# Cross-attention of a small transformer block: two phases with one softmax per row, in place of a running softmax

## The chip, the cores and the metric

The kernel runs on one core of one Trainium2 chip. A core has a matrix engine (TensorE, PE in the rows), a vector engine (VectorE, DVE), an activation engine (ScalarE, ACT), GpSimd (POOL) and SyncE (SP), which here only issues DMAs. The engines run their own instruction streams in order and meet at semaphores. The metric is the device time of one execution in microseconds (us). Before the change it was 133.56 us, the median of 3 runs (132.82 to 136.61).

## The reference, cut to what matters

```python
def _L0_xattn_ref(query, value):                      # 256 queries, 4096 keys, width 256
    scores = jnp.einsum('bqd,bkd->bqk', query, value)
    distribution = jax.nn.softmax(scores, axis=-1)
    return jnp.einsum('bqk,bkd->bqd', distribution, value)

x = x + _L0_xattn_ref(_layernorm(x, axis=-1), ctx_1024)
x = x + _L0_attn_ref(_layernorm(x, axis=-1), L0_attn_w_attn, L0_attn_w_proj)   # 16 heads, causal, position biases
x = x + _L0_ffn_ref(_layernorm(x, axis=-1), L0_ffn_Wg, L0_ffn_W1, L0_ffn_W2, L0_ffn_W3)  # 8 experts
```

`ctx_1024` is 4096 rows of 256 numbers and serves as keys and as values. The change concerns the first of the three lines.

## The kernel before, in words

All data is fp32. The 256 queries are two blocks b of 128 rows, the 4096 keys are eight chunks i of 512. For accuracy each fp32 operand of a product is split into a high part (`_hi`, rounded to the format fp32r that the matrix engine takes in one pass) and a rest (`_lo` = operand - high part), and a product is three matmuls: hi x hi, hi x lo, lo x hi. A tile (i, b) is one chunk against one block. It costs:

- PE: `scores_of` (L837 to L848), 6 matmuls of 512 columns; `transpose_of` (L850 to L857), 4 transposes of the probabilities; `values_of` (L859 to L870), 12 matmuls of 256 columns.
- ACT: `exps` (L692 to L700), exponentials of the scores with the running maximum, with their row sum, and a one-column exponential `shrink` by which older sums must be scaled; `hi_of` (L702 to L708), the high part of the transposed probabilities. Once per chunk also the high part of keys (`split_k`, L674) and of values (`split_v`, L679).
- DVE: `next_max` (L466 to L472), a maximum of the tile and its merge into the running maximum; `lo_of` (L454 to L459); `next_out` (L480 to L491), which rescales the row sum `denom` (L485) and the accumulator `acc` (L490).
- POOL: the low parts of keys and values, `split_lo` (L361 to L370), one instruction each per chunk.

PE, ACT, DVE and POOL each go through the chunks in an order written out by hand, with hardware loops (`Fori`) in the middle. In PE's loop (L886) the scores are one chunk ahead of the values: transpose (i,0), values (i-1,1), scores (i+1,0), transpose (i,1), values (i,0), scores (i+1,1). Two PSUM banks hold scores, two hold transposes, two hold chunk outputs.

All loads are on SP's queue. Keys `kT` and values `v_sb` of all eight chunks have their own space, so their loads (L294 to L304) wait only for the load before them; then come the weights of the later stages (L305 to L314), the 4 MB of `wup_sb` among them. Behind the cross-attention stand `add_attention` (divide, add to x), the statistics of the next layer norm (`norm_stats`, its `rstd` on POOL, `norm_apply`), and the causal attention, whose position biases `bias[:, h]` are 16 multiplications of 128x384 on DVE (`bias_heads`, L445): 3 at the start, 4 after the last `norm_apply`, 5 between the two halves of `mask_k(0, .)` and 4 inside the attention. POOL and DVE share the masking of keys per head (L394 and L552).

Of the kernel before, what the change touches and what calls it, by code (L numbers as in the profile page):

```python
# [9 lines left out]

# [5 lines left out]
FP32 = mybir.dt.float32  # L16
# [5 lines left out]
P = 128  # L22
# [4 lines left out]
L = NCH - 1  # L27
# [17 lines left out]
WARM_BEFORE_NORM_1 = 3  # L45
# [4 lines left out]

EARLY_BIASES, MORE_BIASES, LATE_BIASES = 3, 7, 12
# [15 lines left out]
def build(nc, x, ctx_t, ctx_v, w_qkv, w_proj, w_gate, w_up, w_down, out):  # L67
    es = ExitStack()
    with es:
        def sb(name, shape, dtype=FP32):  # L70
            return es.enter_context(nc.sbuf_tensor(name, shape, dtype))

        def carve(region, size, pattern, **axes):

            part = region[0][:, region[1]:region[1] + size]
            region[1] += size
            return part.rearrange(pattern, **axes)

# [36 lines left out]
        k_lo = sb("k_lo", [P, 2, KC, CH], FP32R)
        v_hi = sb("v_hi", [P, 2, NT, C], FP32R)
        v_lo = sb("v_lo", [P, 2, NT, C], FP32R)
        p_hi = sb("p_hi", [P, TB, NT, P], FP32R)
        p_lo = sb("p_lo", [P, TB, NT, P], FP32R)


        before_up = [wup_sb[:, 4:8].rearrange("p e w k h -> p (e w k h)"), 0]
        before_dn = [wdn_sb[:, 4:8].rearrange("p e k c -> p (e k c)"), 0]
        over_v = [v_sb[:, :, :, :].rearrange("p i n c -> p (i n c)"), 0]
        bias = carve(before_up, NH * 3 * P, "p (h k) -> p h k", h=NH)
        probs = before_up[0][:, before_up[1]:before_up[1] + TB * CH].rearrange("p (b k) -> p b k", b=TB)
        biased = carve(before_up, 3 * 512, "p (s k) -> p s k", s=3)
        aprobsT = carve(before_dn, 2 * 4 * 3 * P, "p (s h m q) -> p s h m q", s=2, h=4, m=3)

        y_T = carve(before_dn, NO * T, "p (o t) -> p o t", o=NO)  # L130
        kM = carve(over_v, NH * T, "p (h k) -> p h k", h=NH)
        k_plain = carve(over_v, 2 * T, "p (m t) -> p m t", m=2)


        UW = 32 * NH // 2
        vpad = carve(over_v, TB * 2 * (UW + HD), "p (k n) -> p k n", k=TB)
        v_slots = [vpad[:, b].rearrange("p (u n) -> p u n", u=2)[:, :, 0:UW].rearrange(
            "p u (m d) -> p u m d", d=32)[:, :, :, 0:HD] for b in range(TB)]
        aprobs = carve(over_v, 3 * 512, "p (s k) -> p s k", s=3)
        q_T = carve(over_v, 2 * T, "p (m t) -> p m t", m=2)  # L140
# [23 lines left out]
        weighted = carve(over_v, TB * E * CAP, "p (b n) -> p b n", b=TB)  # L164
        scatter = carve(over_v, EG * TB * P, "p (g b t) -> p g b t", g=EG, b=TB)
        xg_T = carve(over_v, KC * E * CAP, "p (k n) -> p k n", k=KC)
        act = carve(over_v, EG * H, "p (g h) -> p g h", g=EG)
        h_T = carve(over_v, EG * KH * P, "p (g k n) -> p g k n", g=EG, k=KH)
        y_e = carve(over_v, EG * C, "p (g c) -> p g c", g=EG)
        x_out = carve(over_v, TB * C, "p (b c) -> p b c", b=TB)  # L170
# [3 lines left out]
        s_bank, t_bank, o_bank = banks[0:2], banks[4:6], banks[6:8]  # L174
# [22 lines left out]
        first_kT_loaded = sem("first_kT_loaded")  # L197
        first_v_loaded = sem("first_v_loaded")
        kT_loaded = sem("kT_loaded")
        v_loaded = sem("v_loaded")  # L200
# [16 lines left out]
        scores_ready = sem("scores_ready")  # L217
        chunkmax_ready = sem("chunkmax_ready")
        negmax_ready = sem("negmax_ready")
        probs_ready = sem("probs_ready")  # L220
        shrink_ready = sem("shrink_ready")
        probsT_in_psum = sem("probsT_in_psum")
# [910 lines left out]
```

## Time and profile before

| | before |
|---|---|
| median of 3 runs | 133.56 us (132.82 to 136.61) |
| span of the profiled execution | 134.4 us |
| first score matmul to end of last values matmul | 7.24 to 70.95 us |
| one chunk in the loop | 7.20 us |
| busy in the span: PE, DVE, ACT, POOL | 117.0, 96.3, 68.1, 56.5 us |

The profile is one execution. Starts and durations of instructions are in us from the start of the span; a matmul's duration overlaps the next one's, so the pace of matmuls is read from the distance of their starts. "Idle before" is how long an engine did nothing ahead of an instruction, and behind the arrow stands what it waited for last.

### The profile page before, as it was taken

The numbers are of one execution on the slowest core, as the hardware profiler recorded it, in microseconds if no ns is written. First come the engines' busy times: TensorE is split into PE (matmuls) and PEld (weight loads), VectorE is DVE, ScalarE is ACT, GpSimd is POOL, SyncE is SP. The second block draws the span as 40 slices with busy tenths as digits, with TensorE's granted clock in tenths as the row PEclk, the third lists the DMA queues.
The fourth block names the chain that finished last, engine by engine and source line by source line (L and its number), as shares of the span: only waits on it lengthen the run. The fifth ranks groups of instructions, "written<-read, shape, count | busy, mean of one in ns | idle before, by whom it ended". The sixth has DMA issues, their size and how long they took to land.

```text
span 134.4 us, 2666 instructions
## 1 busy us (share of the span) xinstructions
PE 117.0 (87%) x838; PEld 87.9 (65%) x838; DVE 96.3 (72%) x260; ACT 68.1 (51%) x171; POOL 56.5 (42%) x56
## 2 busy tenths in 40 slices
PE   5990599998989898998896999998999898799982
PEld 5770489896969697887794956554467577534540
DVE  0899566798988979798958887998867489410312
ACT  3470745866757483938421439989690320415100
POOL 2599075292948577585501799500000330300000
PEclk9999779999999999999999999999999999999999
DMA  4998878879999100059000000000057989300002
GB/s 133 356 369 251 273 274 294 258 226 304 429 441 468 68 0 0 0 156 454 22 0 0 2 0 0 0 5 2 0 141 322 458 351 444 166 0 0 0 5 78
DMA packets 3754, 22.69 MB, mean 169 GB/s; under 512 B 544, under 2 KB 800, under 8 KB 3232
## 3 DMA queue, kind: packets, MB, share of 16 engines
q1 hardware_dynamic: 3744, 22.55, 44.6%
q8 instruction: 6, 0.10, 0.3%
q14 instruction: 4, 0.03, 0.1%
HBM read 22.29 MB, written 0.26 MB: 168 GB/s over the span
## 4 chain that ended last, share of the span: by engine, by line
DVE 45%; PE 30%; ACT 10%; issue 8%; DMA 2%; POOL 2%; ACTq 1%; DVEq 1%
DVE denom L485 7%; DVE wup_sb L448 7%; PE bank L1047 5%; DVE negmax L471 5%; DVE chunkneg L468 3%; ACT p_hi L707 3%; PE bank L918 3%; PE bank L1062 3%; DVE v_sb L552 3%; DVE wup_sb L563 2%; ACT v_sb L768 2%; PE bank L948 2%; DVE acc L490 2%; DMA x_sb<-x_in 2%; PE bank L965 2%
## 5 line engine op out<-in xcount | busy, mean ns | idle before, releaser
L365 POOL TENSOR_TENSOR k_lo<-wdn_sb,k_hi (+1 forms) x7 | 16.9, 2414 | 16.1 <-ACT k_hi L677 16.0
L369 POOL TENSOR_TENSOR v_lo<-v_sb,v_hi (+1 forms) x8 | 19.5, 2441 | 4.1 <-ACT v_hi L682 4.1
L696 ACT ACTIVATE wup_sb<-bank,negmax 128x512 f32<-128x512 f32 x16 | 11.0, 687 | 16.7 <-DVE negmax L471 11.7
L866 PE MATMUL bank<-v_hi,p_hi 128*128 128x256 f32 (+1 forms) x64 | 19.4, 303 | 0.0
L867 PE MATMUL bank<-v_lo,p_hi 128*128 128x256 f32 (+1 forms) x64 | 18.0, 282 | 0.0
L868 PE MATMUL bank<-v_hi,p_lo 128*128 128x256 f32 (+1 forms) x64 | 18.0, 282 | 0.0
L855 PE MATMUL bank<-ident,wup_sb 128*128 128x128 f32 x64 | 10.5, 289 | 7.6 <-ACT wup_sb L696 7.6
L332 POOL TENSOR_TENSOR rstd<-vareps,power 128x1 f32<-128x1 f32 x6 | 3.4, 573 | 29.7 <-DVE vareps L422 29.6
L855 PEld LDWEIGHTS bank<-ident,wup_sb 128*128 128x128 f32 x64 | 7.6, 146 | 12.0 <-ACT wup_sb L696 10.9
L457 DVE TENSOR_TENSOR p_lo<-bank,p_hi 128x512 fp32r<-128x512 f32 x16 | 11.0, 686 | 6.3 <-ACT p_hi L707 6.3
L768 ACT ACTIVATE v_sb<-wup_sb,nmax 128x128 f32<-128x128 f32 (+1 forms) x32 | 14.1, 443 | 2.2 <-DVE nmax L563 2.2
L828 PE MATMUL bank<-ident 128*128 128x128 f32 x86 | 13.0, 309 | 1.7 <-POOL ident L326 1.6
L828 PEld LDWEIGHTS bank<-ident 128*128 128x128 f32 x86 | 12.1, 218 | 2.3 <-POOL ident L326 1.6
L844 PE MATMUL bank<-k_hi,q_hi 128*128 128x512 f32 (+1 forms) x32 | 13.4, 418 | 0.0
L707 ACT ACTIVATE p_hi<-bank 128x512 fp32r<-128x512 f32 x16 | 9.5, 593 | 7.2 <-PE bank L855 7.1
L845 PE MATMUL bank<-k_lo,q_hi 128*128 128x512 f32 (+1 forms) x32 | 13.1, 409 | 0.0
L846 PE MATMUL bank<-k_hi,q_lo 128*128 128x512 f32 (+1 forms) x32 | 13.0, 405 | 0.0
L918 PE MATMUL bank<-v_sb 128*128 128x512 f32 x24 | 12.3, 601 | 0.2 <-DVE v_sb L552 0.2
L866 PEld LDWEIGHTS bank<-v_hi,p_hi 128*128 128x128 f32 x64 | 12.3, 192 | 0.2 <-DVE p_lo L457 0.2
L867 PEld LDWEIGHTS bank<-v_lo,p_hi 128*128 128x128 f32 x64 | 12.2, 191 | 0.0
L868 PEld LDWEIGHTS bank<-v_hi,p_lo 128*128 128x128 f32 x64 | 12.1, 190 | 0.0
L485 DVE SCALAR_TENSOR_TENSOR denom<-denom,shrink,rowsum 128x1 f32<-128x1 f32 x14 | 11.2, 797 | 0.0
(120 smaller groups left out, 236.9 us busy)
## 6 DMA issues: line engine op xcount, KB each, us to landing
wup_sb<-w_up SPq DMA_DIRECT2D x2, 4096.0 KB, 14.6
wdn_sb<-ctx_t SPq DMA_DIRECT2D x8, 512.0 KB, 4.1
v_sb<-ctx_v SPq DMA_DIRECT2D x8, 512.0 KB, 4.5
wdn_sb<-w_down SPq DMA_DIRECT2D x2, 2048.0 KB, 10.6
wqkv_sb<-w_qkv SPq DMA_DIRECT2D x1, 768.0 KB, 7.2
x_sb<-x_in SPq DMA_DIRECT2D x1, 256.0 KB, 2.8
wproj_sb<-w_proj SPq DMA_DIRECT2D x1, 256.0 KB, 7.3
x_out_dram<-v_sb SPq DMA_DIRECT2D x2, 128.0 KB, 1.8
```

The costliest lines, as they stand in the source:

```text
L365: nc.gpsimd.tensor_tensor(k_lo[:, i % 2], kT[:, i], k_hi[:, i % 2].bitcast(FP32), ALU.subtract).then_inc(k_lo_ready, 1)
L369: nc.gpsimd.tensor_tensor(v_lo[:, i % 2], v_sb[:, i], v_hi[:, i % 2].bitcast(FP32), ALU.subtract).then_inc(v_lo_ready, 1)
L485: nc.vector.scalar_tensor_tensor(denom[:, b:b + 1], denom[:, b:b + 1], shrink[:, b, bass.ds(i, 1)], rowsum[:, b, bass.ds(i, 1)], ALU.mult, ...
L707: nc.scalar.activation(p_hi[:, b].rearrange("p n q -> p (n q)"), t_bank[b][:, :], ACT.Copy).then_inc(p_hi_ready, 1)
L768: last = nc.scalar.activation(aprobs[:, n % 3, m * keys:(m + 1) * keys], biased[:, n % 3, m * keys:(m + 1) * keys], ACT.Exp, bias=nmax[:, ...
L828: nc.tensor.matmul(bank[:, 0:P], ident[:, :], ident[:, :], start=True, stop=True)
L844: nc.tensor.matmul(s_bank[b][:, :], q_hi[:, k, cols], k_hi[:, i % 2, k], start=(k == 0), stop=False)
L855: last = nc.tensor.transpose(t_bank[b][:, n * P:(n + 1) * P], probs[:, b, n * P:(n + 1) * P], ident[:, :])
L866: nc.tensor.matmul(o_bank[b][:, 0:C], p_hi[:, b, n], v_hi[:, i % 2, n], start=(n == 0), stop=False)
L867: nc.tensor.matmul(o_bank[b][:, 0:C], p_hi[:, b, n], v_lo[:, i % 2, n], start=False, stop=False)
L868: last = nc.tensor.matmul(o_bank[b][:, 0:C], p_lo[:, b, n], v_hi[:, i % 2, n], start=False, stop=(n == NT - 1))
L918: nc.tensor.matmul(as_bank[n % 3][:, :], q_T[:, h // HPT, b * P:(b + 1) * P], kM[:, h:h + len(heads), 0:keys], start=True, stop=True).then ...
```

## The change

The cross-attention becomes two phases. In the first, PE makes all 16 score tiles; ACT copies each from PSUM to SBUF (`keep_scores`), where all of them stay (`scores_sb`), and DVE takes the tile's maximum from SBUF (`chunk_max`). `row_max` reduces the eight maxima of a block to one. In the second phase ACT writes exponentials over the kept scores with that one maximum, and the value products of all chunks add up in one PSUM bank per block. `v_hi` has two more columns, ones and zeros, so that the row sum is column 256 of the product. `shrink`, `denom` and `acc`, the merging of maxima and the row sums are gone. `S_TILES` and `P_TILES` give the order of tiles in the phases.

Work moves between engines: low parts of keys and values go from POOL to DVE (`split_k_lo`, `split_v_lo`), the high part of values from ACT to POOL (`split_v_hi`), all 16 bias multiplications from DVE to POOL. Keys pass through three input buffers (KB), values through two (`v_in`), and the split values through four (VB); the transposes have three PSUM banks and three `p_hi`/`p_lo` buffers (PB). Values from chunk 2 on are loaded behind the weights, and the later weights are loaded earlier than before. The loops are unrolled, and the second norm's transpose of block 0 stands before the last values tile, in place of three warming matmuls.

```diff
@@ constants
+S_TILES = [(i, b) for i in range(NCH - 2) for b in range(TB)] + [(i, b) for b in range(TB) for i in (NCH - 2, NCH - 1)]
+P_TILES = [(0, 0), (1, 0)] + [t for i in range(2, NCH) for t in ((i, 0), (i - 2, 1))] + [(NCH - 2, 1), (NCH - 1, 1)]
+SB, PB, KB, VB = 4, 3, 3, 4
...
@@ SyncE
-            for i in range(2, NCH):
-                sync.wait_ge(kT_loaded, (i - 1) * 16)
-                sync.dma_start(kT[:, i], ctx_t[i]).then_inc(kT_loaded, 16)
-                sync.wait_ge(v_loaded, (i - 1) * 16)
-                sync.dma_start(v_sb[:, i], ctx_v[i]).then_inc(v_loaded, 16)
+            for i in range(KB, NCH):
+
+                sync.wait_ge(k_lo_ready, i - KB + 1)
+                sync.dma_start(k_in[:, i % KB], ctx_t[i]).then_inc(k_loaded[i % KB], 16)
             sync.dma_start(wqkv_sb[:, :, :], w_qkv).then_inc(wqkv_loaded, 16)
...
+            sync.dma_start(wup_lo[:, :, :, :, :], w_up[:, 0:4]).then_inc(wup_loaded[0], 16)
+            for i in range(2, NCH):
+
+                sync.wait_ge(v_lo_ready, i - 1)
+                sync.dma_start(v_in[:, i % 2], ctx_v[i]).then_inc(v_loaded[i % 2], 16)
...
@@ GpSimd
+            def split_v_hi(i):
+                pool.wait_ge(v_loaded[i % 2], 16 * (i // 2 + 1))
+                if i >= VB:
+
+                    pool.wait_ge(values_ready, P_AT[i - VB, 1] + 1)
+                nc.gpsimd.tensor_copy(v_hi[:, i % VB, :, 0:C], v_in[:, i % 2]).then_inc(v_hi_ready, 1)
+
+            pool.wait_ge(rel_ready, 2)
+            for i in range(2):
+                split_v_hi(i)
+            bias_heads(0, 10)
+            for i in range(2, NCH):
+                split_v_hi(i)
+                bias_heads(8 + i, 9 + i)
...
@@ VectorE
+            def chunk_max(i, b):
+                n = S_AT[i, b]
+                dve.wait_ge(scores_kept_s, n + 1)
+                nc.vector.tensor_reduce(chunkneg[:, b, i:i + 1], scores_sb[:, b, i], AX.X, ALU.max,
+                                        negate=True).then_inc(chunkmax_ready, 1)
...
+            for i in range(NCH - 2):
+                split_k_lo(i + 1)
+                for b in range(TB):
+                    chunk_max(i, b)
+            split_k_lo(NCH - 1)
+            chunk_max(NCH - 2, 0)
+            split_v_lo(0)
+            chunk_max(NCH - 1, 0)
+            row_max(0)
+            chunk_max(NCH - 2, 1)
+            split_v_lo(1)
+            chunk_max(NCH - 1, 1)
+            row_max(1)
+            lo_of(*P_TILES[0])
+            for h in range(1, TB * NCH):
+                if h % 2 and (h + 3) // 2 < NCH:
+                    split_v_lo((h + 3) // 2)
+                lo_of(*P_TILES[h])
...
@@ ScalarE
+            for i in range(NCH - 2):
+                split_k_hi(i + 2)
+                for b in range(TB):
+                    keep_scores(i, b)
+            keep_scores(NCH - 2, 0)
+            keep_scores(NCH - 1, 0)
+            exps(*P_TILES[0])
+            exps(*P_TILES[1])
+            keep_scores(NCH - 2, 1)
+            exps(*P_TILES[2])
+            hi_of(*P_TILES[0])
+            keep_scores(NCH - 1, 1)
...
@@ TensorE
+            for h in range(TB * NCH):
+                values_of(*P_TILES[h])
+                if h + PB < TB * NCH:
+                    transpose_of(*P_TILES[h + PB])
+                if h == TB * NCH - 2:
+                    norm_T(1, 0)
```

What this does to the order of work is seen best on two engines. DVE before, from the first tile of its loop body (a bracket names the semaphores that an instruction waits for; ISA and REGISTER_ALU rows are the loop's register work):

```order
L457 TENSOR_TENSOR p_lo<-bank,p_hi 128x512 [waits p_hi_ready]
L482 ISA
L483 REGISTER_ALU [waits shrink_ready]
L485 ISA [waits denom_ready,probs_ready]
L485 SCALAR_TENSOR_TENSOR denom<-denom,shrink,rowsum 128x1
L490 SCALAR_TENSOR_TENSOR acc<-acc,shrink,bank 128x256 [waits acc_ready,chunk_out_ready]
L467 ISA
L468 TENSOR_REDUCE chunkneg<-bank 128x1 [waits scores_ready]
L470 REGISTER_ALU
L471 ISA [waits chunkmax_ready]
L471 TENSOR_TENSOR negmax<-chunkneg,negmax 128x1
```

DVE now, from the end of the first phase into the second (L476 and L482 are the low parts of keys and values, L488 a tile's maximum, L493 the row's, L498 the low part of probabilities):

```order
L476 TENSOR_TENSOR k_lo<-k_in,k_hi 128x1024 [waits k_hi_ready]
L488 TENSOR_REDUCE chunkneg<-scores_sb 128x1 [waits scores_kept_s]
L482 TENSOR_TENSOR v_lo<-v_in,v_hi 128x1024 [waits v_hi_ready]
L488 TENSOR_REDUCE chunkneg<-scores_sb 128x1 [waits scores_kept_s]
L493 TENSOR_REDUCE negmax<-chunkneg 128x1 [waits chunkmax_ready]
L488 TENSOR_REDUCE chunkneg<-scores_sb 128x1 [waits scores_kept_s]
L482 TENSOR_TENSOR v_lo<-v_in,v_hi 128x1024 [waits v_hi_ready]
L488 TENSOR_REDUCE chunkneg<-scores_sb 128x1 [waits scores_kept_s]
L493 TENSOR_REDUCE negmax<-chunkneg 128x1 [waits chunkmax_ready]
L498 TENSOR_TENSOR p_lo<-bank,p_hi 128x512 [waits p_hi_ready]
L482 TENSOR_TENSOR v_lo<-v_in,v_hi 128x1024 [waits v_hi_ready]
L498 TENSOR_TENSOR p_lo<-bank,p_hi 128x512 [waits p_hi_ready] x2
```

The rescaling is gone from a tile, the split of a chunk's keys or values has come in, and the low part of the second tile of the phase stands behind the low part of value chunk 2.

POOL before, its loop over chunks and what stood behind it:

```order
L365 TENSOR_TENSOR k_lo<-wdn_sb,k_hi 128x1024
L369 ISA [waits v_hi_ready]
L369 ISA
L369 TENSOR_TENSOR v_lo<-v_sb,v_hi 128x1024
L378 REGISTER_ALU
L378 COMPARE_AND_BRANCH
```

POOL now, in the same stretch (L403 is the high part of a value chunk, L396 one bias multiplication):

```order
L403 CAST v_hi<-v_in 128x4x256 [waits v_loaded1]
L396 TENSOR_SCALAR bias<-rel 128x384 x10
L403 CAST v_hi<-v_in 128x4x256 [waits v_loaded0]
L396 TENSOR_SCALAR bias<-rel 128x384
L403 CAST v_hi<-v_in 128x4x256 [waits v_loaded1]
L396 TENSOR_SCALAR bias<-rel 128x384
L403 CAST v_hi<-v_in 128x4x256 [waits values_ready,v_loaded0]
```

Two subtractions per chunk have left POOL; a copy per chunk and the bias multiplications have come, and from chunk 4 on the copy waits for PE's values.

## Rows read from the trace of the kernel before

**Rows 1.** By stretch: length, busy us PE PEld DVE ACT POOL, clock, DMA, GB/s.
```profile
33.20:40.40 7.20, 6.72 (x46) 5.81 (x45) 6.30 (x11) 4.79 (x11) 4.80 (x2) 1.00 1.02 416
...
16.00:18.00 2.00, 2.00 (x6) 1.41 (x6) 0.69 (x1) 1.12 (x2) 0.80 (x1) 0.50 0.81 297
```

**Rows 2.** Timeline, one loop turn: start, duration, instruction, idle before it.
```profile
35.99 2.44 POOL L369 TENSOR_TENSOR v_lo<-v_sb,v_hi  x1
...
36.46 0.28 PE L867 MATMUL bank<-v_lo,p_hi 128*128 x1
...
36.58 0.28 PE L868 MATMUL bank<-v_hi,p_lo 128*128 x1
...
37.24 1.21 DVE L471 TENSOR_TENSOR negmax<-chunkneg,negmax 128x1 f32 x1 [0.19 <-DVE chunkneg L468]
...
38.61 0.69 ACT L696 ACTIVATE wup_sb<-bank,negmax 128x512 f32<-128x512 f32 x1 [1.74 <-DVE negmax L471]
```

**Rows 3.** Chain that ended last: start, us; four transposes and one score matmul.
```profile
21.78 0.44 PE bank L855 x4
23.64 0.23 PE bank L844
```

**Rows 4.** Groups by line and shape: count, busy us, mean ns, idle before.
```profile
L457 DVE TENSOR_TENSOR p_lo<-bank,p_hi 128x512 fp32r<-128x512 f32 x16 | 11.0, 686 | 6.3 <-ACT p_hi L707 6.3
L468 DVE TENSOR_REDUCE chunkneg<-bank 128x1 f32<-128x512 f32 x14 | 9.5, 680 | 2.2 <-PE bank L846 2.2
...
L707 ACT ACTIVATE p_hi<-bank 128x512 fp32r<-128x512 f32 x16 | 9.5, 593 | 7.2 <-PE bank L855 7.1
...
L677 ACT ACTIVATE k_hi<-wdn_sb 128x1024 fp32r<-128x1024 f32 x3 | 3.2, 1053 | 2.7 <-DMA wdn_sb<-ctx_t 2.7
```

**Rows 5.** Timeline of the start.
```profile
6.18 0.67 DVE L437 TENSOR_TENSOR k_lo<-wdn_sb,k_hi 128x512 fp32r<-128x512 f32 x1
...
7.24 0.49 PE L844 MATMUL bank<-k_hi,q_hi 128*128 128x512 f32 x1
...
8.43 2.55 DVE L448 TENSOR_SCALAR wup_sb<-rel 128x384 f32<-128x384 f32 x1
...
10.72 2.47 POOL L369 TENSOR_TENSOR v_lo<-v_sb,v_hi 128x1024 fp32r<-128x1024 f32 x1
...
14.88 0.66 PE L855 MATMUL bank<-ident,wup_sb 128*128 128x128 f32 x4 [4.59 <-ACT wup_sb L696]
```

**Rows 6.** SP's issue of value chunk 2; issue to landing of the 4 MB loads.
```profile
9.34 0.33 SPq L304 DMA_DIRECT2D v_sb<-ctx_v  x1
...
DMA to landing us min/median/max: 12.6/14.6/16.6
```

**Rows 7.** POOL: a memset by group; the masking line's min/median/max ns.
```profile
L384 POOL MEMSET v_sb<- 128x1088 f32 x1 | 1.0, 1012 | 0.1
...
L394 POOL TENSOR_SCALAR v_sb<-v_sb,headmask x16: 598/606/1101, 75.2 to 85.2; 128x128 f32<-128x128 f32 x16
```

**Rows 8.** Timeline behind the cross-attention.
```profile
70.67 0.28 PE L868 MATMUL bank<-v_hi,p_lo 128*128 128x256 f32 x1
...
72.45 0.48 DVE L526 SCALAR_TENSOR_TENSOR x_sb<-acc,rdenom,x_sb 128x256 f32<-128x256 f32 x1
...
73.88 0.55 POOL L332 TENSOR_TENSOR rstd<-vareps,power 128x1 f32<-128x1 f32 x1 [1.98 <-DVE vareps L422]
74.47 0.41 DVE L427 TENSOR_SCALAR xn<-x_sb,meanvar,rstd 128x256 f32<-128x256 f32 x1 [0.67 <-POOL rstd L332]
...
74.80 1.25 DVE L448 TENSOR_SCALAR wup_sb<-rel 128x384 f32<-128x384 f32 x4
...
76.78 1.60 DVE L448 TENSOR_SCALAR wup_sb<-rel 128x384 f32<-128x384 f32 x5
...
77.43 0.38 ACT L754 ACTIVATE v_sb<-bank 128x256 f32<-128x256 f32 x1 [0.51 <-PE bank L935]
...
87.54 1.15 DVE L448 TENSOR_SCALAR wup_sb<-rel 128x384 f32<-128x384 f32 x4
```

More of the change, by code:

```diff
@@ L115, in build @@
[L115 to L125, printed above, removed]
@@ new lines, in build, with carve @@
+        room = region(KB * KC * CH)
+        k_in = at("k_in", [P, KB, KC, CH], room)
+        p_hi = at("p_hi", [P, PB, NT, P], room, FP32R)
+        p_lo = at("p_lo", [P, PB, NT, P], room + PB * CH * 4, FP32R)
+        split_probs = room
+        room = region(VB * NT * (2 * C + 2))
+        v_hi = at("v_hi", [P, VB, NT, C + 2], room, FP32R)
+        v_lo = at("v_lo", [P, VB, NT, C], room + VB * NT * (C + 2) * 4, FP32R)
+        over_v_first = room
+        over_v = [over_v_first]
+        def carve(name, shape, region_at):
+            first = region_at[0]
+            region_at[0] += (math.prod(shape[1:]) * 4 + 63) // 64 * 64
+            return at(name, shape, first)
@@ L196, in build @@
         x_loaded = sem("x_loaded")
[L197 to L200, printed above, removed]
+        k_loaded = [sem(f"k_loaded{j}") for j in range(KB)]
+        v_loaded = [sem(f"v_loaded{j}") for j in range(2)]
         wqkv_loaded = sem("wqkv_loaded")
@@ L443, in _, with split_k_lo @@
                                         ALU.subtract).then_inc(q_lo_ready, 1)
-            def bias_heads(first, end):
-                for h in range(first, end):
-                    nc.vector.tensor_scalar(bias[:, h], rel[:, :], SLOPES[h], None, ALU.mult)
-            dve.wait_ge(rel_ready, 2)
-            bias_heads(0, EARLY_BIASES)
+            def split_k_lo(i):
+                dve.wait_ge(k_hi_ready, i + 1)
+                nc.vector.tensor_tensor(k_lo[:, i % KB], k_in[:, i % KB], k_hi[:, i % KB].bitcast(FP32),
+                                        ALU.subtract).then_inc(k_lo_ready, 1)
@@ L834, in _, with scores_half @@
             keep_warm(banks[7], WARM_BEFORE_SCORES)
[L837 to L839 removed]
+            def scores_half(i, b, k):
+                n = S_AT[i, b]
                 cols = slice(b * P, (b + 1) * P)
[L841 to L848 removed]
@@ new lines, in scores_half, with room_for_scores @@
+                nc.tensor.matmul(s, q_hi[:, k, cols], k_lo[:, i % KB, k], start=False, stop=False)
+                last = nc.tensor.matmul(s, q_lo[:, k, cols], k_hi[:, i % KB, k], start=False, stop=(k == KC - 1))
+                if k == KC - 1:
+                    last.then_inc(scores_in_psum, 1)
+            def room_for_scores(i, b):
+                n = S_AT[i, b]
+                pe.wait_ge(k_lo_ready, i + 1)
+                if n >= SB:
+                    pe.wait_ge(scores_kept_s, n - SB + 1)
@@ new lines, in transpose_of, with values_of @@
+            def transpose_of(i, b):
+                h = P_AT[i, b]
+                pe.wait_ge(probs_ready, h + 1)
+                if h >= PB:
+                    pe.wait_ge(p_lo_ready, h - PB + 1)
+                for n in range(NT):
+                    last = nc.tensor.transpose(t_bank[h % PB][:, n * P:(n + 1) * P],
+                                               scores_sb[:, b, i, n * P:(n + 1) * P], ident[:, :])
+                last.then_inc(probsT_in_psum, 1)
+            def values_of(i, b):
+                h = P_AT[i, b]
+                pe.wait_ge(p_lo_ready, h + 1)
+                pe.wait_ge(v_lo_ready, i + 1)
+                hi, lo = o_bank[b][:, 0:C + 2], o_bank[b][:, 0:C]
+                for n in range(NT):
+                    nc.tensor.matmul(hi, p_hi[:, h % PB, n], v_hi[:, i % VB, n], start=(i == 0 and n == 0), stop=False)
+                    nc.tensor.matmul(lo, p_hi[:, h % PB, n], v_lo[:, i % VB, n], start=False, stop=False)
+                    last = nc.tensor.matmul(hi, p_lo[:, h % PB, n], v_hi[:, i % VB, n], start=False,
+                                            stop=(i == NCH - 1 and n == NT - 1))
+                last.then_inc(values_ready, 1)
```

417 lines of the change are left out of this document (145 added, 272 removed).

## The prediction

> **What bounds the kernel now.** I read the busy times by stretch first, then the timeline of one loop turn, then the chain that ended last. A turn of the loop takes 7.20 us, and PE is busy for 6.72 of them; no other engine passes 6.3 [rows 1]. Counted by the distance of starts, a score matmul takes 0.23 us, four transposes 0.44 [rows 3], a values matmul 0.12 [rows 2]. A turn has 12, 8 and 24 of them: 2.77 + 0.88 + 2.86 = 6.5 us. So PE is within 0.7 us per turn of its own floor, and this is all that a better order can win per turn. The reader should see what the 0.7 is: POOL's split of values runs from 35.99 to 38.43, and DVE's one-column merge of the maximum, started at 37.24, lasts 1.21 us and ends with it. ACT's exponential waited 1.74 us for that [rows 2]. The rest of the loss before the loop is one hole: PE waits 4.59 us up to 14.88 [rows 5], since a DVE multiplication that takes 1.15 / 4 = 0.3 us alone [rows 8] took 2.55 beside POOL [rows 5], and behind it PE's clock stood at half speed, 1.2 GHz [rows 1].
>
> **Phase one.** The first score starts at 7.24 [rows 5] as before. Sixteen tiles of 6 matmuls are 16 x 1.39 = 22.2 us, to 29.4 if PE never waits. What could make it wait is the loop over chunks: the copy of a tile's scores 0.6 (as ACT's p_hi), the maximum 0.65 (rows 4 show 0.68 at a pace of 0.61), then the low part of the next but one chunk's keys, 1.2 (0.67 for half the size [rows 5] plus 512 more elements at 1 ns), and 0.3 of handovers: 2.75, against 2.77 for the two tiles that PE has meanwhile. It just fits. It does not fit twice. Key chunk 3 queues behind key 2 and both first values: value chunk 1 landed at 9.34 [rows 6], one load more ahead of it and one behind put key 3 at about 12.1; ACT's copy 1.05 [rows 4], two tile copies that stand behind it, two maxima and the low part end at 16.6, so PE's seventh tile starts 1.2 late. At the end, tile (7,0) stands one tile earlier than its chunk's low part comes and waits 1.4. Half a tile's transposes lie between the last tiles; scores end near 33.3.
>
> **The turn between the phases.** Tile (7,0) ends at 29.6; copy, maximum and row maximum give 31.4. ACT then has two exponentials (0.65 each), a copy, an exponential, a high part and the last copy (0.6 to 0.65 each): 35.2. DVE's last maximum, the row maximum of block 1 and the first low part (0.65 + 0.35 + 0.7), in DVE's order all ahead of the first values, end at 36.9. PE is idle for about 2.3 us before that. I take no clock loss for it, since the hole behind which the clock fell was twice as long, 4.59 us [rows 5]; the bound on the other side is the whole 2.00 us that rows 1 show at half speed, and somewhat more, 1.7 us lost.
>
> **Phase two.** PE needs 16 x 1.43 for values, 13 x 0.44 for transposes and 0.25 for the norm's: 28.9, to 65.8. ACT (0.65 + 0.6 a tile) and DVE (0.6 and every other tile 1.2) have less. The two extra columns are 2 in 256. But two waits come in.
>
> First, value chunk 2 is loaded behind the weights. Its space is free at 30, but key 7 goes out at 19.5, the 4 MB at 21.6, and a 4 MB load landed 12.6 to 16.6 us after issue, 14.6 in the middle [rows 6]: 36.2, and 1.2 for the chunk itself, 37.4. POOL's copy, DVE's subtraction and the low part of tile 1 queued behind it (1.3 + 1.2 + 0.7) end at 40.6, where PE would have been ready at 38.8: 1.8 lost (none at 12.6, 3.8 at 16.6).
>
> Second, from chunk 4 on POOL may only copy when values tile h = 2i-5 has read the old chunk; DVE's subtraction and, queued behind it, the low part for values tile 2i-3 must follow. From the end of one to the start of the other: result and handover 0.25, copy 1.3, subtraction 1.2, low part 0.7, handover 0.05 = 3.5. PE has 0.44 + 1.43 + 0.44 = 2.3 to do. So 1.17 lost per chunk, four times: 4.7. That gives back most of what the phases win: the end is 65.8 + 1.8 + 4.7 = 72.3, against 70.95 - 0.16 = 70.8 before by the same count (start 70.67 and 0.12) [rows 8].
>
> The copy's price is in no row. POOL's memset of 1088 columns takes 1.01, its two-operand subtraction of 1024 takes 2.44 [rows 7, 2]; so 1.0 to 2.4. A copy has one input, and beside DVE a masking of 128 columns grew from 0.60 to 1.10 while DVE's four biases only grew from 1.15 to 1.25 [rows 7, 8]: POOL's access to memory in it is short, most of it is start-up. I take 1.3, nearer the memset. The Trainium skill ("GPSIMD Engine Reference", 4.1 Engine selection) says one-input work runs there at about line rate; by its 1.2 GHz that is an estimate of 0.85 plus start-up, and the sum would be 0.8 lower; no row here shows it.
>
> **Behind it.** The row sum comes out of the matmul: reciprocal and division start 0.4 after the last matmul, where before DVE stood 1.8 behind the start at 70.67 with two rescalings, at 72.45 [rows 8]. Now 72.3 + 0.4 = 72.7: 0.25 later than before. The nine biases ahead of the attention go: the second mask waited for them until 78.38, though its keys were there at 77.81 [rows 8], which is 0.55. The four at 87.54, 1.15 us [rows 8], stood in the chain, but PE is nearly full there; I take 0.7 (0 to 1.15). On POOL they hide: ten in phase one, six beside phase two, with POOL waiting there anyway. Later weights come earlier; nobody waited for them. Sum on the profiled execution: 0.25 - 0.55 - 0.7 = -1.0, 134.4 to 133.4. The median lies 0.84 below that span, so 132.6.
>
> **The rivals.**
> - *PE-bound (0.31).* The copy is a memset's 1.0 (-1.2), the weights land in 12.6 (-1.8), and phase one keeps PE's pace but for one of its two holes (-1.3): 132.6 - 4.3 = 128.3. For it: PE's own sum has 6.5 us of waits over its floor in phase two alone. Against it: DVE's order puts the low part behind the chunk split, whatever the copy costs.
> - *The port (0.18), ending slower.* In the trace a DVE instruction with SBUF operands waits for a whole POOL one, 1.21 and 2.55 us [rows 2, 5]. Behind every value copy stands a bias on POOL, with no wait. If it gets going before DVE's subtraction does, that waits for all of it. A bias is three times the masked size: between 0.6 and 1.8, near 0.9. Five times 0.9 is 4.5: 137.1; it decides from 0.75 each. Against it: DVE starts 0.04 after POOL ends (74.43 to 74.47 [rows 8]), and at 10.72 to 10.98 DVE went first although POOL's next instruction had begun [rows 5]. Where the forecast has the bias giving way, the Trainium skill ("SBUF - State Buffer", SBUF: two separate sides) speaks against it: whichever starts first holds the shared port for the whole instruction. By that rule this rival comes true if the bias counts as started.
> - *A slow copy (0.09).* At the subtraction's rate, 2.4, each of five turns costs 1.1 more: 138.1. It takes 0.75 each to reach the slower side too.
> - *A cold clock* after the idle before phase two adds up to 1.7: 134.3, still within 2%, and lies in the forecast's own range, 131.0 to 135.5.
>
> **How the numbers follow.** Forecast 0.42, the others 0.31, 0.18 and 0.09. About 2% is what a measurement of this kernel can tell from no change: 130.9 and 136.2. Faster 0.31, within 0.42, slower 0.27. The range goes from PE-bound, 128.3, to the slow copy: 128.3 to 138.0.
>
> **What would show it.** Phase one right: no score tile waits over 0.3 us but the seventh and (7,0), first values at 36 to 38. Second wait right: PE idle about 1.2 us before values tiles 5, 7, 9 and 11, each released by DVE's p_lo, with the v_lo before it released by POOL. The port right: that v_lo lasts 2 us instead of 1.2 and ends as a bias ends. Slow copy right: L403 over 2 us. The forecast is wrong altogether if the clock falls in phase two more than once, or if key loads, not DVE, set phase one's pace.

## The result, and the profile after

The changed kernel takes 137.11 us (median of 4 runs, 135.98 to 137.69) where the kernel before takes 134.06 in the same comparison (4 runs, 132.82 to 136.61). The ratio is 1.0241 with a 95% interval of 1.016 to 1.0323: slower beyond the noise, though whether by more than 2% the interval leaves open. The forecast was 132.6, a little faster than before; the range of 128.3 to 138.0 holds the time. The ratios here leave out runs more than 1.5% above the fastest of their kernel, so they are not always the quotient of the two medians shown.

| | before | after |
|---|---|---|
| median | 134.06 us | 137.11 us |
| span of the profiled execution | 134.4 us | 135.3 us |
| spans of other runs | 131.2 to 136.4 (20 runs) | 134.0, 135.2, 135.7 |
| second division of the attention | 72.45 | 74.14 |
| from there to the end | 61.95 | 61.2 |
| busy: PE, DVE, ACT, POOL | 117.0, 96.3, 68.1, 56.5 | 117.3, 80.3, 65.1, 52.7 |

PE does the same work, DVE 16 us less, and the kernel is slower. So the question is not how much work there is but where PE waits. The timeline of PE in the changed kernel, only the rows with a wait of some length, starts, durations, and in brackets the idle time before and what ended it:

```profile
27.49 0.50 PE L809 MATMUL bank<-k_hi,q_hi 128*128 128x512 f32 x1 [1.16 <-DVE k_lo L476]
...
35.84 0.39 PE L837 MATMUL bank<-v_hi,p_hi 128*128 128x258 f32 x1 [1.91 <-DVE p_lo L498]
...
40.31 0.39 PE L837 MATMUL bank<-v_hi,p_hi 128*128 128x258 f32 x1 [2.33 <-DVE p_lo L498]
...
50.69 0.39 PE L837 MATMUL bank<-v_hi,p_hi 128*128 128x258 f32 x1 [1.06 <-DVE p_lo L498]
...
55.76 0.39 PE L837 MATMUL bank<-v_hi,p_hi 128*128 128x258 f32 x1 [1.07 <-DVE p_lo L498]
...
60.55 0.39 PE L837 MATMUL bank<-v_hi,p_hi 128*128 128x258 f32 x1 [0.78 <-DVE p_lo L498]
...
65.36 0.39 PE L837 MATMUL bank<-v_hi,p_hi 128*128 128x258 f32 x1 [0.79 <-DVE p_lo L498]
```

Every long wait of the second phase ends with DVE's low part of the exponentials, `p_lo`. It is not slow itself. The groups of the profile page (count, busy us, mean ns, idle before and its releaser) show what stands ahead of it:

```profile
L837 PE MATMUL bank<-v_hi,p_hi 128*128 128x258 f32 x64 | 20.1, 314 | 7.9 <-DVE p_lo L498 7.9
...
L482 DVE TENSOR_TENSOR v_lo<-v_in,v_hi 128x1024 fp32r<-128x1024 f32 x8 | 10.4, 1295 | 14.8 <-POOL v_hi L403 14.8
...
L403 POOL CAST v_hi<-v_in 128x1024 fp32r<-128x1024 f32 x8 | 8.3, 1041 | 22.0 <-DMA v_in<-ctx_v 11.3
...
L498 DVE TENSOR_TENSOR p_lo<-bank,p_hi 128x512 fp32r<-128x512 f32 x16 | 10.4, 682 | 1.8 <-ACT p_hi L685 1.7
```

DVE stands idle for 14.8 us ahead of its value splits, waiting for POOL's copy, while ACT has long finished the `p_hi` of the low part that is queued behind the split. POOL in turn waits, first for the load and then for PE's values; value chunk 2 and value chunk 4 as examples:

```profile
37.36 1.04 POOL L403 CAST v_hi<-v_in 128x1024 fp32r<-128x1024 f32 x1 [10.46 <-DMA v_in<-ctx_v]
...
47.44 1.04 POOL L403 CAST v_hi<-v_in 128x1024 fp32r<-128x1024 f32 x1 [3.37 <-PE bank L839]
```

The third thing is PE's clock, by stretch (stretch, length, busy us of PE, PEld, DVE, ACT, POOL, granted clock, DMA share, GB/s):

```profile
41.00:42.00 1.00, 1.00 (x9) 1.00 (x8) 0.18 (x1) 0.00 (x0) 0.92 (x2) 0.79 0.87 340
42.00:43.00 1.00, 1.00 (x7) 1.00 (x6) 1.00 (x2) 0.00 (x0) 1.00 (x1) 0.50 0.27 107
43.00:44.00 1.00, 1.00 (x7) 1.00 (x7) 0.88 (x3) 0.86 (x2) 1.00 (x1) 0.50 0.00 0
44.00:45.00 1.00, 1.00 (x6) 1.00 (x6) 0.46 (x1) 0.35 (x1) 0.07 (x1) 0.51 0.94 225
45.00:75.00 30.00, 26.30 (x218) 25.35 (x217) 14.99 (x24) 11.96 (x21) 11.41 (x9) 1.00 0.44 169
```

Behind the holes of 1.91 and 2.33 us, with 2 us of matmuls between them, PE ran at 1.2 GHz for over 3 us. The shortfall of the four rows is 0.21 + 0.50 + 0.50 + 0.49 = 1.70 us of full-speed work, all with PE busy.

At the other end of the queue stand POOL's bias and DVE's split, which the rivals were about. One turn in which the bias began first, and one in which the split did:

```profile
48.44 1.17 POOL L396 TENSOR_SCALAR bias<-rel 128x384 f32<-128x384 f32 x1
48.52 1.52 DVE L482 TENSOR_TENSOR v_lo<-v_in,v_hi 128x1024 fp32r<-128x1024 f32 x1 [4.05 <-POOL v_hi L403]
...
58.67 1.23 DVE L482 TENSOR_TENSOR v_lo<-v_in,v_hi 128x1024 fp32r<-128x1024 f32 x1 [2.37 <-POOL v_hi L403]
58.72 2.21 POOL L396 TENSOR_SCALAR bias<-rel 128x384 f32<-128x384 f32 x1
```

In four of six turns DVE began first and the bias was held (2.21 us against 1.17). In the other two the bias began less than 0.1 us earlier, and the split took 1.52 instead of 1.23. So there is a price for the port that POOL and DVE share, 0.3 us twice.

### The profile page after: what moved, and what is told of

Its sections match the earlier page's. It is cut to its first block, busy times and chain, and to the rows that moved or that the text cites. A ratio compares the mean times of both kernels' runs of the same rounds, so it can differ in the third digit from the quotient of the medians.

```text
span 135.3 us, 2296 instructions
## 1 busy us (share of the span) xinstructions
PE 117.3 (87%) x832; PEld 89.0 (66%) x832; DVE 80.3 (59%) x215; ACT 65.1 (48%) x149; POOL 52.7 (39%) x67
## 4 chain that ended last, share of the span: by engine, by line
PE 41%; DVE 26%; DMA 11%; ACT 8%; issue 6%; POOL 6%; POOLq 0%
DMA v_in<-ctx_v 6%; ACT aprobs L736 6%; DVE v_lo L482 6%; PE bank L1009 5%; PE bank L837 4%; POOL v_hi L403 4%; DMA k_in<-ctx_t 3%; PE bank L839 3%; PE bank L838 3%; PE bank L1024 3%; PE bank L927 3%; PE bank L910 2%; PE bank L809 2%; DVE p_lo L498 2%; PE bank L880 2%
## 5 line engine op out<-in xcount | busy, mean ns | idle before, releaser
L837 PE MATMUL bank<-v_hi,p_hi 128*128 128x258 f32 x64 | 20.1, 314 | 7.9 <-DVE p_lo L498 7.9
L396 POOL TENSOR_SCALAR bias<-rel 128x384 f32<-128x384 f32 x16 | 25.1, 1569 | 1.1
L482 DVE TENSOR_TENSOR v_lo<-v_in,v_hi 128x1024 fp32r<-128x1024 f32 x8 | 10.4, 1295 | 14.8 <-POOL v_hi L403 14.8
L839 PE MATMUL bank<-v_hi,p_lo 128*128 128x258 f32 x64 | 18.6, 291 | 0.0
L838 PE MATMUL bank<-v_lo,p_hi 128*128 128x256 f32 x64 | 18.5, 289 | 0.0
L403 POOL CAST v_hi<-v_in 128x1024 fp32r<-128x1024 f32 x8 | 8.3, 1041 | 22.0 <-DMA v_in<-ctx_v 11.3
L736 ACT ACTIVATE aprobs<-biased,nmax 128x128 f32<-128x128 f32 (+1 forms) x32 | 14.1, 442 | 1.7 <-DVE nmax L554 1.7
L809 PE MATMUL bank<-k_hi,q_hi 128*128 128x512 f32 x32 | 13.1, 409 | 1.2 <-DVE k_lo L476 1.2
L488 DVE TENSOR_REDUCE chunkneg<-scores_sb 128x1 f32<-128x512 f32 x16 | 10.8, 683 | 5.5 <-ACT scores_sb L672 5.4
L838 PEld LDWEIGHTS bank<-v_lo,p_hi 128*128 128x128 f32 x64 | 12.7, 199 | 0.0
L811 PE MATMUL bank<-k_hi,q_lo 128*128 128x512 f32 x32 | 12.5, 390 | 0.0
L810 PE MATMUL bank<-k_lo,q_hi 128*128 128x512 f32 x32 | 12.5, 390 | 0.0
L678 ACT ACTIVATE scores_sb<-scores_sb,negmax 128x512 f32<-128x512 f32 x16 | 11.3, 715 | 2.0 <-DVE negmax L493 2.0
L880 PE MATMUL bank<-kM,q_T 128*128 128x512 f32 x24 | 12.1, 600 | 0.0
L498 DVE TENSOR_TENSOR p_lo<-bank,p_hi 128x512 fp32r<-128x512 f32 x16 | 10.4, 682 | 1.8 <-ACT p_hi L685 1.7
```

The source lines that it names most:

```text
L396: nc.gpsimd.tensor_scalar(bias[:, h], rel[:, :], SLOPES[h], None, ALU.mult).then_inc(bias_ready, 1)
L403: nc.gpsimd.tensor_copy(v_hi[:, i % VB, :, 0:C], v_in[:, i % 2]).then_inc(v_hi_ready, 1)
L482: nc.vector.tensor_tensor(v_lo[:, i % VB], v_in[:, i % 2], v_hi[:, i % VB, :, 0:C].bitcast(FP32), ALU.subtract).then_inc(v_lo_ready, 1)
L498: nc.vector.tensor_tensor(p_lo[:, h % PB].rearrange("p n q -> p (n q)"), t_bank[h % PB][:, :], p_hi[:, h % PB].rearrange("p n q -> p (n q) ...
L736: last = nc.scalar.activation(aprobs[:, n % 3, m * keys:(m + 1) * keys], biased[:, n % 3, m * keys:(m + 1) * keys], ACT.Exp, bias=nmax[:, ...
L809: nc.tensor.matmul(s, q_hi[:, k, cols], k_hi[:, i % KB, k], start=(k == 0), stop=False)
```

## Experiment 1: is it the order of DVE, or the late load?

The theory: the holes in phase two come from DVE's order, in which the low part for the next values tile stands behind a value split that is waiting for POOL. The rival: what costs is the load of value chunk 2, queued behind 4 MB of weights, with the clock that falls behind it. Three kernels, all from the changed one. The first moves one load.

```diff
-            sync.dma_start(wup_lo[:, :, :, :, :], w_up[:, 0:4]).then_inc(wup_loaded[0], 16)
             for i in range(2, NCH):
...
+            sync.dma_start(wup_lo[:, :, :, :, :], w_up[:, 0:4]).then_inc(wup_loaded[0], 16)
```

> The changed kernel, with one line moved: SyncE issues the 4 MB load of the first up-weights behind the last value chunk instead of ahead of value chunk 2. Theory A (value chunk 2 is late because of the weights in the queue): PE's idle of 2.33 us before its second values tile falls under 0.5, value chunk 2 lands near 33, and the half-speed stretch of PE behind it (about 3.3 us, 1.3 us lost) may go too: 2.0 to 3.6 us faster than the changed kernel, span 131.7 to 133.3. Rival R (the hole is a matter of DVE's and POOL's order or of the port between them, not of the load): copy and subtraction end no earlier, span 135 again.

Measured: 136.39 us, ratio to before 1.0204 (1.0069 to 1.034), against 1.0241 for the change itself: no gain that can be told, where the theory of the load had asked for 2.0 to 3.6 us. Its timelines of PE, POOL and DVE:

```profile
35.91 0.39 PE L837 MATMUL bank<-v_hi,p_hi 128*128 128x258 f32 x1 [2.13 <-DVE p_lo L498]
...
48.16 0.39 PE L837 MATMUL bank<-v_hi,p_hi 128*128 128x258 f32 x1 [1.06 <-DVE p_lo L498]
...
32.35 1.04 POOL L403 CAST v_hi<-v_in 128x1024 fp32r<-128x1024 f32 x1 [5.62 <-DMA v_in<-ctx_v]
...
71.64 0.48 DVE L505 SCALAR_TENSOR_TENSOR x_sb<-bank,rdenom,x_sb 128x256 f32<-128x256 f32 x1
```

The copy of value chunk 2 starts at 32.35 instead of 37.36 and the hole of 2.33 is gone; the second division comes at 71.64, 2.50 earlier. But the span is 134.5, only 0.8 shorter. The stretches (the same columns as above) show why: half speed came again behind the single hole of 2.13, and a second time in the last stage, where the changed kernel had full speed.

```profile
37.00:38.00 1.00, 1.00 (x7) 1.00 (x6) 0.96 (x2) 1.00 (x3) 0.14 (x1) 0.50 0.11 45
...
116.00:117.00 1.00, 1.00 (x8) 0.27 (x4) 0.00 (x0) 0.00 (x0) 0.00 (x0) 0.50 0.06 16
117.00:118.00 1.00, 1.00 (x8) 0.27 (x4) 0.00 (x0) 0.00 (x0) 0.00 (x0) 0.50 0.00 0
```

From the division to the end it took 62.9 us instead of 61.2, so 1.7 was given back. The instructions there are the same in both kernels. So moving the load did what was expected up to the division, and the clock took most of it back.

The second kernel swaps two statements in DVE's second phase.

```diff
             for h in range(1, TB * NCH):
+                lo_of(*P_TILES[h])
                 if h % 2 and (h + 3) // 2 < NCH:
                     split_v_lo((h + 3) // 2)
-                lo_of(*P_TILES[h])
```

> The changed kernel, with two lines swapped in DVE's second phase: the low part of values tile 2i-3 stands ahead of the low part of value chunk i instead of behind it. Theory A (PE waits for a low part that only queues behind the chunk's split): the four idles of 1.06, 1.07, about 0.9 and 0.79 us before values tiles 5, 7, 9 and 11 go, the first hole before tile 1 gets shorter by up to 1.9 us, since that tile's low part no longer waits for chunk 2 (tile 1 is of chunk 1): 3.5 to 5.5 us faster than the changed kernel, span 130 to 132. Rival R (POOL's copy and DVE's split are slow because they hold each other up at the port): tile 2i-2 waits instead of tile 2i-3, and at most 1.5 us is won.

Measured: 129.83 us, ratio to before 0.9691 (0.9531 to 0.9852), 7.3 us under the changed kernel's median, which was taken in another comparison. The group of the first values matmuls on its page:

```profile
L837 PE MATMUL bank<-v_hi,p_hi 128*128 128x258 f32 x64 | 20.0, 313 | 1.9 <-DVE p_lo L498 1.9
```

The timelines of PE, POOL and DVE:

```profile
35.42 0.58 PE L837 MATMUL bank<-v_hi,p_hi 128*128 128x258 f32 x1 [1.91 <-DVE p_lo L498]
...
48.16 1.04 POOL L403 CAST v_hi<-v_in 128x1024 fp32r<-128x1024 f32 x1 [1.58 <-PE bank L839]
51.90 1.04 POOL L403 CAST v_hi<-v_in 128x1024 fp32r<-128x1024 f32 x1 [1.57 <-PE bank L839]
...
66.34 0.48 DVE L505 SCALAR_TENSOR_TENSOR x_sb<-bank,rdenom,x_sb 128x256 f32<-128x256 f32 x1
```

The idle time ahead of values tiles falls from 7.9 to 1.9 us. All four holes are gone and so is the one of 2.33: value chunk 2 lands as late as before, its copy starts at 37.01, and PE does not wait for it in this trace. POOL's copies come every 3.75 us (48.16 to 51.90), which is PE's own pace for two values tiles. So the late load cost what it did through the queue of DVE. The port falls as the cause too: the splits of 1.52 us and the biases of 2.21 us are still in this trace.

One thing is hidden here. Behind the 1.91 hole PE runs at half speed for 3.4 us, 35.4 to 38.8, which costs 1.7. Values tile 2, the first that needs value chunk 2, starts at 40.72, and its low part was ready near 39.9. Without the half speed PE would have come for it near 39.0 (an estimate, 40.72 - 1.7) and waited 0.9. So about half of what the slow clock costs here would have been a wait for the load anyway; the last kernel of experiment 3, in which the clock stays up, does wait there. The third kernel has both edits.

> The changed kernel with both edits of the two kernels before it. Theory A: PE's values phase has no idle over 0.3 us and no half-speed stretch: 3.9 + 2.3 + 1.3 = 7.5 us less than the changed kernel, span 127.5 to 129. If the two are one and the same slack, the sum is smaller than the two alone added. Rival R: no faster than the better of the two by more than 0.5.

Measured: 130.65 us, ratio 0.9778 (0.9676 to 0.988). The earlier load brings nothing beside the swap, as the rival expected; the intervals of the two overlap. The theory had asked for a phase without half speed, and the 3.4 us of it behind the 1.91 hole are there in this kernel too. So the case in which the earlier load should help, with the clock up, was not measured.

## Experiment 2: what did the kernel before lose at its start?

The baseline had a hole of 4.59 us and a half-speed stretch [rows 5, 1], which the change removes together with DVE's early biases. How much of a comparison is that? The kernel before, with no early bias on DVE:

```diff
-EARLY_BIASES, MORE_BIASES, LATE_BIASES = 3, 7, 12
+EARLY_BIASES, MORE_BIASES, LATE_BIASES = 0, 7, 12
```

> The kernel before, with one number changed: EARLY_BIASES 0 instead of 3, so that the three bias multiplications at the start, which took 5.2 us on DVE beside POOL's splits, stand behind the second layer norm instead (three more there at 0.3 us each). Theory A (the 4.59 us hole and the half-speed stretch behind it are the largest single loss of the kernel before and owe to these three): the hole shrinks to about 1 us and the clock stays up: 3 to 4.5 us won, 0.9 given back, so 2 to 3.6 us faster than the kernel before. Rival R2 (key and value loads, with 4 landings of 512 KB ahead, set the pace there): under 1 us is won.

Measured: 134.65 us over 10 runs, ratio 1.0051 (0.999 to 1.0112): the same time. Its timelines of PE and DVE:

```profile
10.78 0.66 PE L855 MATMUL bank<-ident,wup_sb 128*128 128x128 f32 x4 [0.31 <-ACT wup_sb L696]
...
69.14 0.48 DVE L526 SCALAR_TENSOR_TENSOR x_sb<-acc,rdenom,x_sb 128x256 f32<-128x256 f32 x1
...
75.97 0.92 DVE L552 TENSOR_SCALAR v_sb<-v_sb,headmask 128x128 f32<-128x128 f32 x4
```

The hole is gone and the division comes 3.31 us earlier than in rows 8, but the biases that are now behind the attention delay the next stage (from the division to the end 62.9 us, before 61.95), and the span is 132.0. The theory had expected 2 to 3.6 us and missed; the rival had the size right but not its reason, since the hole did shrink, from 4.59 to 0.31, and the loads did not hold it open. Why so little is won is seen when the kernel before is profiled once more:

> The kernel before, unchanged, profiled once more. If the profiled execution that the prediction was worked on had a half-speed stretch that most runs don't have, this one has a span of 131 to 133 us with the clock at its upper level behind the hole at the start; if the hole always brings it, the span is 134 to 135 again.

```profile
12.79 0.66 PE L855 MATMUL bank<-ident,wup_sb 128*128 128x128 f32 x4 [2.42 <-ACT wup_sb L696]
...
70.62 0.48 DVE L526 SCALAR_TENSOR_TENSOR x_sb<-acc,rdenom,x_sb 128x256 f32<-128x256 f32 x1
```

Here the hole is 2.42 us, the clock does not fall while PE has work, and the span is 132.6. Against this execution the division without early biases comes only 1.48 us earlier, and 0.9 of it is given back behind it. So the profiled execution that I predicted from, 134.4 us, was one of the long ones: among 20 more runs of the same kernel, those with a mean clock of 0.995 or more have spans of 131.2 to 132.6, and those below 132.0 to 136.4. All runs of all kernels here show a time 1.7 to 2.9 us above their span; the four of the changed kernel 1.8 to 2.0.

## Experiment 3: the clock, the port, and the rest

Two more kernels from the changed one. The first keeps PE busy with throwaway matmuls in the two long holes, 14 pairs before values tile 0 and 18 before tile 1, so as to price the clock alone.

```diff
+            pe.wait_ge(scores_kept_s, TB * NCH - 2)
+            keep_warm(banks[1], 14)
             for h in range(TB * NCH):
+                if h == 1:
+                    keep_warm(banks[1], 18)
                 values_of(*P_TILES[h])
```

> The changed kernel, with 14 warming matmuls of 128 columns ahead of the first values tile and 18 ahead of the second, in the two stretches where PE was idle for 1.91 and 2.33 us (as many as fit by 0.11 each); nothing is left out. Theory A (the half-speed stretch from 41.6 to 45.0 follows from these two idles): PE's clock stays at its upper level through the values phase and the end of the phase comes 1.2 to 1.5 us earlier; the two holes and the four later ones stay. Rival R (the clock falls for another reason, or is not on the path since PE waits for POOL's copies afterwards anyway): within 0.3 us of the changed kernel.

Measured: 139.02 us, ratio 1.0391 (1.0276 to 1.0506): no faster, where 1.2 to 1.5 us had been expected. Its timeline of PE, and the division:

```profile
33.38 3.29 PE L796 MATMUL bank<-ident 128*128 128x128 f32 x28
36.42 0.36 PE L837 MATMUL bank<-v_hi,p_hi 128*128 128x258 f32 x1
...
38.38 4.18 PE L796 MATMUL bank<-ident 128*128 128x128 f32 x36
42.31 0.36 PE L837 MATMUL bank<-v_hi,p_hi 128*128 128x258 f32 x1
...
74.55 0.48 DVE L505 SCALAR_TENSOR_TENSOR x_sb<-bank,rdenom,x_sb 128x256 f32<-128x256 f32 x1
```

The clock stayed at 1.00 in this trace. But the fillers were longer than the holes. They had been counted at 0.11 us each, and each filler matmul is two of the rows above, so 14 of them took 3.29 us, 0.23 each. Tile 1 starts at 42.31 instead of 40.31. From there to the division it takes 32.24 us, in the changed kernel 33.83. So full speed is worth 1.59 us, close to the 1.70 read from the stretches, and 2.00 was paid for it. As a price of the clock the experiment works; as a remedy it failed by its own size. The trace explains 0.4 us of the loss (division at 74.55 against 74.14); why the median lies 1.9 above the changed kernel's, in another comparison, it does not show.

The second takes the biases out from behind the copies, all 16 ahead of value chunk 2.

```diff
-            bias_heads(0, 10)
+            bias_heads(0, 16)
             for i in range(2, NCH):
                 split_v_hi(i)
-                bias_heads(8 + i, 9 + i)
```

> The changed kernel, with the six bias multiplications that POOL makes behind value chunks 2 to 7 moved in front of chunk 2, to the ten that it makes in the first phase. The port theory (a bias that has started holds up DVE's subtraction): the two subtractions of 1.52 us become 1.22, chunk 3's copy no longer waits for the bias of 2.21 us (1.1 us), and 0.6 to 1.5 us are won. Theory A (the four holes are the serial chain copy, subtraction, low part behind PE's values, and the port adds 0.3 to two of them): 0.6 us at most, the four holes still 0.8 us each.

Measured: 138.44 us, ratio 1.0306 (1.0221 to 1.039). Its lines are numbered one lower. Timelines of POOL and PE:

```profile
38.88 1.97 POOL L403 CAST v_hi<-v_in 128x1024 fp32r<-128x1024 f32 x1 [0.19 <-DMA v_in<-ctx_v]
...
40.61 0.39 PE L836 MATMUL bank<-v_hi,p_hi 128*128 128x258 f32 x1 [2.78 <-DVE p_lo L497]
...
50.70 0.39 PE L836 MATMUL bank<-v_hi,p_hi 128*128 128x258 f32 x1 [0.78 <-DVE p_lo L497]
...
55.50 0.39 PE L836 MATMUL bank<-v_hi,p_hi 128*128 128x258 f32 x1 [0.79 <-DVE p_lo L497]
```

The holes before these two tiles shrink from 1.06 and 1.07 to 0.78 and 0.79, and no split lasts longer than 1.23 us. That is the port's whole price in these turns: 0.3 us in two of them, 0.6 in all. From the start of tile 1 to the division it takes 33.28 us, in the changed kernel 33.83. The hole before tile 1 is 2.78 instead of 2.33, since value chunk 2 landed 0.3 later, and the copy behind it, begun while DVE's split ran, took 1.97 instead of 1.04. With the kernel that has the swap this takes the port as a cause of the slowdown off the table. The kernel as a whole isn't faster: the second division comes 0.25 earlier, at 73.89, and the last stage has a second half-speed stretch again, as in experiment 1.

Last, a kernel that puts together what the others taught: the swap of the second kernel, `split_k_lo` of the last key chunk and the first low part each moved ahead of maxima that nobody waits for yet, and 8 pairs of fillers before the values.

```diff
                 split_k_lo(i + 1)
+                if i == NCH - 3:
+                    split_k_lo(NCH - 1)
...
             split_v_lo(1)
+            lo_of(*P_TILES[0])
             chunk_max(NCH - 1, 1)
```

> The kernel of e2_low_part_first with three edits more: key chunk 7's low part goes ahead of the two maxima of chunk 5 (PE waited 1.13 us for it), the first tile's low part goes ahead of the last maximum (PE waited 1.91 us, of which 0.65 is that maximum), and 8 warming matmuls fill the rest of that hole. Theory A: 1.1 + 0.65 us and 0.5 to 1.3 for the clock, 2 to 3 us faster than e2_low_part_first, span about 125, 5% faster than the kernel before. Rival R (the maximum of the last tile, and with it block 1's exponentials, becomes late by as much): the first saves 1.1, the second nothing.

Measured: 129.54 us over 5 runs, ratio 0.9654 (0.9578 to 0.9729). Expected was a span of about 125, and it is 128.5: a miss. The kernel beats the one before clearly, and the swap alone by nothing that can be told. Timelines of PE, POOL and ACT (values rows are L838 here; the first two begin tiles 0 and 1, the third tile 2):

```profile
35.63 0.36 PE L838 MATMUL bank<-v_hi,p_hi 128*128 128x258 f32 x1
...
37.96 0.39 PE L838 MATMUL bank<-v_hi,p_hi 128*128 128x258 f32 x1 [0.22 <-DVE p_lo L498]
...
41.65 0.39 PE L838 MATMUL bank<-v_hi,p_hi 128*128 128x258 f32 x1 [1.56 <-DVE p_lo L498]
...
38.69 1.04 POOL L403 CAST v_hi<-v_in 128x1024 fp32r<-128x1024 f32 x1 [10.52 <-DMA v_in<-ctx_v]
...
13.42 1.06 ACT L668 ACTIVATE k_hi<-k_in 128x1024 fp32r<-128x1024 f32 x1 [1.73 <-DMA k_in<-ctx_t]
```

What was meant to be mended is mended: the wait of 1.13 us for the last keys and the hole of 1.91 are gone (the second is filled), the clock stays up, and the first values start only 0.2 us later than in the swap's trace (35.42), although ACT got key chunk 3 at 13.42, there at 11.88, with the same loads issued in the same order. But tile 2, the first that needs value chunk 2, now waits 1.56 us: POOL's copy of that chunk waited 10.52 us for the load and starts at 38.69, in the swap's trace at 37.01. Tile 2 starts 0.93 us later than there, the division comes 0.94 later (67.28 against 66.34), and the spans differ by 0.9.

So the landing of value chunk 2 is a floor that none of the three edits moves. Tile 2 starts 2.96 us behind POOL's copy of its chunk; from the 37.01 of the swap's trace it could have started at 39.97 (an estimate), only 0.75 ahead of the 40.72 that it has there. That is the most that was to be won of the 2 to 3 us expected, and in this execution, the longest of the five (the others have spans of 127.3 to 127.8, the swap's four 127.1 to 129.1), the load came too late even for that. It was late from the first keys on; what decides that is open. The kernel to try next is this one with the weights behind the values; it was not run.

## Why the prediction was wrong

**Right.** The mechanism of the second wait, its place, its releaser and its price. Predicted were four holes before values tiles 5, 7, 9 and 11, costing 4.7 us; they are there, each released by `p_lo`. With them two tiles take 5.07 (50.69 to 55.76), 4.79 and 4.81 us, without them 3.75, so a hole costs 1.0 to 1.3 us, predicted 1.17. From the start of tile 1 to the last division predicted were 72.7 - 40.6 = 32.1, and measured 33.83 - 1.70 for the clock = 32.1. Value chunk 2 was to land at 37.4; POOL's copy starts at 37.36. Tile 1 was to start at 40.6 and starts at 40.31. Phase one came out 1.1 us better than its sum: the seventh score tile waits under 0.2 us (predicted 1.2), tile (7,0) waits 1.16 (predicted 1.4), and the values start at 35.84 (predicted 36.9). It brought nothing, since tile 1 had to wait for value chunk 2 in any case. The copy on POOL takes 1.04 us, nearer the memset than the 1.3 I took. The Trainium skill ("GPSIMD Engine Reference", 4.1 Engine selection) has one-input work there at about line rate, and for the copy the trace agrees: 1024 elements in 1.04 us. For the bias multiplication, which has one input too, it does not: 384 elements take 1.17 us.

**The port** was weighed about right. Of the rule of the Trainium skill ("SBUF - State Buffer", SBUF: two separate sides), that whichever starts first holds the shared port for its whole instruction, the trace bears out who is held: the later one, in all six turns. It does not bear out how long, when POOL was first: DVE's split ended 0.43 us behind the bias, far less than its own 1.23.

**Wrong 1: from the span to the median.** "The median lies 0.84 below that span, so 132.6." That is the largest part of the miss. It takes the median of the times from the span of one execution, and a time lies above its own span, by 1.8 to 2.0 us in the changed kernel; the forecast should have read 135.3 from the predicted span of 133.4. That would have been slower than the kernel before, not faster. The step looked harmless because the profiled execution before was a long one: a span of 134.4 belongs to a time of 136.1 to 137.3, and of the three times on hand only the highest, 136.61, lies there. Its start hole and half-speed stretch I had listed myself, and the second profile of the same kernel has less of them (experiment 2). This step is 2.7 of the 4.5 us that the forecast was off.

**Wrong 2: "I take no clock loss for it".** I argued that the hole before the values was half as long as the one behind which the clock had fallen. The bound that I had put beside it, 1.7, is what came. The kernel has two holes close together, 1.91 and 2.33 with about 2 us of matmuls between; and experiment 1 shows half speed behind 1.91 and behind 2.13 alone. In the second profile of the kernel before, the clock stayed up behind 2.42. So in these traces holes of 1.9 to 2.4 us went both ways, and the loss belonged in the sum with a weight of its own. The end of the attention was therefore late: 74.14 against 72.7.

**Wrong 3: the term behind the attention.** Expected was a gain of 1.25 us, 0.55 up to the second mask and 0.7 for the four biases at 87.54. Measured from the division to the end: 61.95 before, 61.2 after, a gain of 0.8. Up to the second mask 5.86 became 5.19, 0.67; so for the four biases only 0.1 is left. On DVE itself they did save 1.17 us: from the masks at 84.38 to the copy at 88.62 it took 4.24 us before, and 3.07 now (85.74 to 88.81). By the end of the attention that was gone again; the work behind must have had other limits, and which ones was not traced.

Put together, from the span of 133.4: tile 1 0.3 earlier, 1.7 for the clock, 0.46 less gained behind the attention make 135.3, the measured span. The rivals: neither the slow copy nor the port came true, and a PE-bound second phase needed what none of its conditions gave, the swap of two statements.

**What stays open**: why half speed came back in the last stage of two kernels (at 116 and at 118 us) behind the same instructions and the same waits that the changed kernel passes at full speed; what moves the landing of the key chunks by over 1 us; and what the last kernel would gain from an earlier load of the values.

## What to carry to other kernels

In an engine that runs in order, put what the next consumer waits for ahead of what is only needed later, above all when the later one has a wait of its own: two statements swapped turned 2.4% slower into 3.1% faster. Taking 16 us of work off DVE, which wasn't the bottleneck, brought nothing by itself; ask of each wait who stands in the queue behind it. A wait that has gone may only be hidden by another loss: with the clock up, the late load was the limit. And before a span is turned into a forecast of the median, find out what the profiled execution has that the median one doesn't.

## What the runs showed of the hardware

- Half speed of TensorE came behind idle times of only 1.91 us (second kernel of experiment 1) and 2.13 us (first kernel), and stayed away behind 2.42 us (the kernel before, profiled again). The stretch in the changed kernel lasted over 3 us and cost 1.6 to 1.7 us; in the second kernel of experiment 1 it lasted 3.4 us.
- A copy with rounding of 128x1024 fp32 takes POOL 1.04 us, and 1.97 once when DVE's split had begun first (experiment 3, the biases first). A multiplication of 128x384 takes it 1.17, and 2.21 when DVE's two-operand split began first; DVE does the same multiplication in 0.3 [rows 8].
- Two executions of one program differ in the length of a hole (4.59 and 2.42 us at the same place), and with it in whether the clock falls. The two spans, 134.4 and 132.6, differ by 1.8 us, and at the division the two are already 1.83 apart. The spans of the kernel before lie between 131.2 and 136.4 us; for how much of that the hole stands was not measured.
